# Layer 1's experts in a four-layer transformer kernel: four of eight chunks routed in 23 blocks instead of dense

## The reference, cut to what matters

```python
def _moe(x, gW, gb, W1, b1, W2, b2):
    xf = x.reshape(-1, d)
    gates = jax.nn.softmax(xf @ gW + gb, axis=-1)
    top2_scores, top2_idx = jax.lax.top_k(gates, 2)
    w = (jax.nn.one_hot(top2_idx, NUM_EXPERTS, dtype=xf.dtype) * top2_scores[..., None]).sum(1)
    h = jax.nn.relu(jnp.einsum('nd,edf->enf', xf, W1) + b1[:, None, :])
    y = jnp.einsum('enf,efd->end', h, W2) + b2[:, None, :]
    out = jnp.einsum('ne,end->nd', w, y)
```

## Time and profile before

| | us |
|---|---|
| timed runs, median (lowest to highest of 3) | 2776.42 (2775.82 to 2781.66) |
| profiled execution, its own time | 2793.7 |
| its span, first to last instruction | 2791.9 |
| TensorE busy | 2617.3 |
| VectorE busy | 2019.3 |
| ScalarE busy | 1664.1 |
| GpSimd busy | 1181.0 |

### The profile page before, as it was taken

The page is one execution under the profiler, slowest core; times in us unless marked ns, Lnnn a source line. Parts: engine busy times, 40 slices in busy tenths (PEclk is TensorE's granted clock), DMA queues, the critical chain, the costliest instruction groups (busy, mean ns, idle before and its releaser), DMA issues.

```text
span 2791.9 us, 67999 instructions
## 1 busy us (share of the span) xinstructions
PE 2617.3 (94%) x24870; PEld 1792.3 (64%) x24870; DVE 2019.3 (72%) x5620; ACT 1664.1 (60%) x4107; POOL 1181.0 (42%) x1620
## 2 busy tenths in 40 slices
PE   5999999998889999999997999999989988999898
PEld 2666666666577666676665555677767765666676
DVE  6988888876544666666666998556678876887675
ACT  3888888884234767777765777543335544334665
POOL 6888888853601566211113454122333321014441
PEclk9999999999999999999999999999999999999999
DMA  3012222112275122111113544000054432435650
GB/s 113 17 54 76 76 75 67 54 37 85 89 219 158 30 45 45 32 39 30 26 32 105 185 136 134 1 1 16 15 160 147 129 92 63 92 78 158 201 165 28
DMA packets 218857, 230.81 MB, mean 83 GB/s; under 512 B 18608, under 2 KB 188272, under 8 KB 216480
## 3 DMA queue, kind: packets, MB, share of 16 engines
q1 hardware_dynamic: 212000, 207.58, 26.9%
q10 hardware_dynamic: 3456, 12.58, 1.4%
q0 software_dynamic: 3072, 6.30, 0.7%
HBM read 165.87 MB, written 75.60 MB: 86 GB/s over the span
## 4 chain that ended last, share of the span: by engine, by line
PE 72%; DVE 12%; ACT 7%; issue 4%; POOL 2%; DMA 2%; SPq 1%; ACTq 0%; another core or an unknown queue 0%; DVEq 0%; POOLq 0%
PE pb L163 64%; ACT big L967 4%; PE pb L663 3%; ACT big L160 2%; DVE big L3015 2%; DVE big L837 2%; PE pb L596 2%; DVE big L236 1%; PE pb L2986 1%; DVE big L3520 1%; PE pb L249 1%; DVE big L820 1%; DVE big L747 1%; POOL hs L1854 1%; DVE big L179 0%
## 5 line engine op out<-in xcount | busy, mean ns | idle before, releaser
L163 PE MATMUL pb<-big 128*128 128x128 f32 (+12 forms) x19624 | 2352.2, 327 | 102.3 <-DVE big L3015 34.5
L163 PEld LDWEIGHTS pb<-big 64*128 64x128 bf16 (+4 forms) x19624 | 1481.4, 144 | 760.4 <-issue 430.8
L160 ACT ACTIVATE big<-pb 128x512 f32<-128x512 f32 (+7 forms) x1481 | 846.4, 620 | 555.1 <-PE pb L163 295.9
L160 ACT ACTIVATE big<-pb,big 128x512 f32<-128x512 f32 (+2 forms) x502 | 276.1, 585 | 426.9 <-PE pb L163 353.7
L3015 DVE TENSOR_REDUCE big<-pb 128x4 f32<-128x1024 f32 (+1 forms) x256 | 277.6, 1087 | 71.4 <-PE pb L163 66.8
L967 ACT ACTIVATE big<-big 128x256 f32<-128x256 f32 x512 | 253.8, 499 | 67.7 <-DVE big L842 66.7
L967 ACT ACTIVATE big<-pb,big 128x128 f32<-128x128 f32 (+1 forms) x512 | 256.8, 527 | 60.1 <-DVE big L822 59.8
L837 DVE CUSTOM_DVE_ANT_0 big<-pb,big 128x256 f32<-128x256 f32 x512 | 186.7, 422 | 96.9 <-PE pb L163 93.6
L187 POOL TENSOR_SCALAR big<-big 128x4 f32<-128x4 f32 (+2 forms) x102 | 26.7, 262 | 542.2 <-DVE big L182 542.1
L174 POOL TENSOR_TENSOR big<-big 128x128 f32<-128x128 f32 x168 | 74.5, 457 | 346.6 <-DVE big L171 346.5
L1046 POOL TENSOR_TENSOR big<-big 128x512 f32<-128x512 f32 x128 | 159.7, 1275 | 139.8 <-DMA big<-recip 139.8
(11 more groups left out here) (211 smaller groups left out, 2452.9 us busy)
## 6 DMA issues: line engine op xcount, KB each, us to landing
parts<-big SPq DMA_DIRECT2D x384, 96.0 KB, 2.5
big<-parts SPq DMA_DIRECT2D x72, 512.0 KB, 4.1
big<-recip SPq DMA_DIRECT2D x128, 256.0 KB, 5.3
big<-comb SPq DMA_DIRECT2D x32, 512.0 KB, 8.0
hs<-in_zero SPq DMA_DIRECT2D x10, 1472.0 KB, 9.1
big<-in_wx SPq DMA_DIRECT2D x31, 450.0 KB, 4.3
parts<-big SPq DMA_DIRECT2D x192, 64.0 KB, 2.1
big<-parts ACTq DMA_DIRECT2D x24, 512.0 KB, 4.6
```

The source lines that it names most:

```text
L160: return e.activation(o, i, f, bias=bias, scale=scale)
L163: return e.matmul(o, l, r_, start=start, stop=stop, skip_group_check=True)
```

## The change

Layer 1's experts become a stage of their own, `routed_ffn`: chunks 0 and 1 dense (units 0 to 15), chunks 2 to 5 routed as 23 blocks of 256 rows (steps 16 to 38), chunks 6 and 7 dense (steps 39 to 54). The routed rows come straight from X1. Ranking and table run beside the first pair, 32 scatters in steps 2 to 13. The table of experts sets which weights a block fetches from a new input `wx1` (642 columns, laid out by expert on the host). Two rows per routed token are gathered from `ys` by `late_ffn_fetch`, 28 of 32 gathers beside the last pair and four in layer 2's attention; `late_ffn_vector`, `late_ffn_scalar` and `late_ffn_gpsimd` combine, normalize and add them four tiles at a time, in steps 45/46 and 49/50 and in steps 2/3 and 12/13 of layer 2's attention. Layer 2's first steps are hosted from step 48 of 55 instead of 55 of 64.

```diff
+        def late_ffn_fetch(e, g):
+            m, k, i = g // 4, g % 4 // 2, g % 2
...
+            if g % 4 == 0 and m >= 3:
+                e.wait_ge(ffn_added, m - 2)
+            t = 2 * m + i
+            at = HOME1[t // 8][:, 8 * k + t % 8:8 * k + t % 8 + 1]
+            e.indirect_dma_start(out=CHOSEN1[m % 3][:, k, i, :], out_offset=None, in_=dr["ys"],
+                                 in_offset=bass.IndirectOffsetOnAxis(ap=at, axis=0)).then_inc(chosen_in[m % 3], 16)
+        def late_ffn_vector(e, c):
...
+            for i, a in enumerate(rows):
+                n = 4 * c + i
+                x = e.scalar_tensor_tensor(out=a[:, 0, :], in0=a[:, 0, :], scalar=SHARE1[:, 0, n:n + 1], in1=X1[:, 8 + n, :],
+                                           op0=ALU.mult, op1=ALU.add)
...
+        def late_ffn_scalar(e, c):
+            e.wait_ge(ffn_rstd, c + 1)
+            for i in range(4):
+                a = CHOSEN1[(2 * c + i // 2) % 3][:, 0, i % 2, :]
+                x = act(e, a, a, ACT.Identity, LNMR[:, i:i + 1], LRS[:, i:i + 1])
+            x.then_inc(ffn_normed, 1)
+        def late_ffn_gpsimd(e, c):
+            e.wait_ge(ffn_mean, c + 1)
...
+            e.tensor_tensor(LRS, LRS, EPS[:, 0:4], ALU.pow).then_inc(own.sem, own.up())
...
+            e.wait_ge(ffn_normed, c + 1)
+            two = lambda a: a.unsqueeze(1).to_broadcast([128, 2, 128])
+            for m in (2 * c, 2 * c + 1):
+                a, b = CHOSEN1[m % 3][:, 0], 4 + m
+                for w, op in ((two(LNW[:, 256:384]), ALU.mult), (two(LNW[:, 384:512]), ALU.add), (two(GA[:, b, 128:256]), ALU.mult)):
+                    e.tensor_tensor(a, a, w, op).then_inc(own.sem, own.up())
+                    e.wait_ge(own.sem, own.n)
+                e.tensor_tensor(X[:, 2 * b:2 * b + 2, :], X[:, 2 * b:2 * b + 2, :], a, ALU.add).then_inc(ffn_added, 1)
+        def routed_ffn():
+            k, E = 1, 8
+            DENSE, ROUTED = (0, 1, 6, 7), (2, 3, 4, 5)
+            NB1 = 23
+            T0, T1 = 16, 16 + NB1
+            T = T1 + 16
...
+            modulated_at, guests_at = T0 + 12, T - 7
...
+            scatters = {t: [(m, three[m % 3]) for m in range(3 * (t - first), min(3 * (t - first) + 3, 16))]
+                        for first in (2, 8) for t in range(first, first + 6)}
+            gathers = {T1 + 1 + 2 * m + i: range(4 * m + 2 * i, 4 * m + 2 * i + 2) for m in range(7) for i in range(2)}
+            combined_at = {T1 + 6: 0, T1 + 10: 1}
...
+            def tensor_block_up(e, j):
...
+                for f in range(2):
+                    t = mm(e, bk[:, 256 * f:256 * f + 256], WB[J % 4][:, 128 * f:128 * f + 128], HTB[J % 3], True, True)
...
+            def vector_block_down(e, j):
+                y, J = slots["y", T0 + j], NBLK + j
+                bk = empty(e, y)
+                e.wait_ge(y_stored[J % 2], 16 * (J // 2))
+                e.tensor_tensor(YB[J % 2], bk[:, 0:256].rearrange("p (k c) -> p k c", k=2),
+                                WB[J % 4][:, 514:642].unsqueeze(1).to_broadcast([128, 2, 128]), ALU.add).then_inc(y.free, 1)
...
+                e.wait_ge(table_made, 2)
+                for j in range(4):
+                    sync_weights(e, j)
+                e.wait_ge(scattered, 16 * (48 + 32))
+                for j in range(4):
+                    sync_rows(e, j)
+                for j in range(NB1 + 1):
+                    if 1 <= j and j + 3 < NB1:
+                        sync_rows(e, j + 3)
+                    if 1 <= j and j + 3 < NB1:
+                        sync_weights(e, j + 3)
+                    if j >= 1:
+                        sync_store(e, j - 1)
...
         in narrow_attention, k == 2:
-                    found += [(c, piece) for at, piece in (((2, "normed0"), (4, "normed1"), (7, "turn")) if b % 2 else
-                                                           ((2, "stats0"), (4, "stats1"))) if at == i]
+                                                           (((5, "stats0"), (6, "stats1")) if causal else ((2, "stats0"), (4, "stats1")))) if at == i]
+                return [(c, p) for c, first in ((2, 2), (3, 12)) for p, at in (("sum", 0), ("norm", 1)) if causal and first + at == t]
+                    if causal and t in (5, 6):
+                        for g in range(18 + 2 * t, 20 + 2 * t):
+                            late_ffn_fetch(e, g)
-                    if k == 2 and b == 5:
-                        e.wait_ge(gated, 8 + 32 * (k - 1))
+                    if k == 2 and b == 11:
+                        e.wait_ge(ffn_added, 8)
+                        e.wait_ge(gated, 24)
                         second_gates(e, k)
-                 moe(1, 8, X1A.rearrange("p (t c) -> p t c", c=128)), narrow_attention(2), ...
+                 routed_ffn(), narrow_attention(2), ...
```

680 lines of the change are left out of this document (658 added, 22 removed).

## The result

The changed kernel took 2790.61 us in the median of seven runs (2785.56 to 2798.59), the kernel before 2777.87 us beside it (2772.55 to 2781.66). The ratio is 1.0049, 95% interval 1.0035 to 1.0063: 13 us slower, clearly told from no change. Measured again later beside other runs of before it was 1.0062 (1.0046 to 1.0079). The forecast was 2769 us, 7 us less than before; the sign was wrong, the time lies inside the range. Its chances were 0.49 for faster and 0.31 for slower.

What follows compares the result with a forecast made beforehand. TensorE alone was taken to set the pace. Terms: -124.3 + 57.5 + 8 + 5 - 6 + 7 + 24 + 21.5 = -7.3 us, from the median 2776.42 to 2769 us; 8-in-10 range 2740 to 2796.

Steps and rivals of the forecast that it cites:

- At nothing: List of edits put at no cost: shared own-semaphores, moved statistics, later load of the second gates, host's table of weights.
- The blocks: Layer 1's 23 routed blocks: 2.5 us each, 57.5 us, plus 5 for gates of chunks 6 and 7 holding VectorE.
- the pieces: Transposes and gate logits of chunks 6 and 7, 6 us, said to fit into TensorE's spare time beside the blocks: -6.
- the store loop of 2.5 us: Layer 1's blocks: with two buffers YB, eviction waits for the store of two blocks earlier, setting 2.5 us a block.
- Rival 2: Blocks at layer 0's pace, store landing at 4.3 us or more, 2.8 to 3.1 us a block; chance 0.28.
- Rival 3: Stores land near 1.8 us, blocks run at TensorE's 2.0 us, 11.5 us less, 2757 us; chance 0.07.
- The first block: Hand-over to the routed blocks: last scatter 5 us too late, 2 more at low clock, +7 us; ends 0 and 11.
- The join: Last dense pair to layer 2's first score: TensorE stands 24 us behind GpSimd's 45 us of work; ends 14 and 30.
- Rival 1: GpSimd's queue is hidden: the 24 us and half of layer 2's loss don't appear, 2735 or 2741 us; chance 0.20.
- Layer 2's early steps: Layer 2's attention: late normalizations, sums and gathers delay negated maxima, splits and exponentials, +21.5 us; ends 10 and 30.
- the blocks' 71 us: Upper end for layer 1's 23 blocks, at 3.08 us each, layer 0's own pace after its first wait.
- GpSimd's 30: Upper end of TensorE's wait for GpSimd's work beside the last dense pair, forecast at 24 us.

Runs made afterwards that it cites:

- gates_load_late: Changed kernel with the load of the next layer's gates issued after the last block's store; ratio 1.0038 to the kernel before.
- three_buffers: Changed kernel with three result buffers YB instead of two in layer 1's blocks; ratio 1.0067 to the kernel before.
- one_multiply: Changed kernel without the product with ln2's weight and the sum with its bias in each late normalization; ratio 1.0020 to the kernel before.
- late_spread: Changed kernel, statistics back in steps 2 and 4, layer 2's two late combinations in steps 22 to 28 and 38 to 44, last gathers in 32, 33; ratio 1.0030 to before.
- after_again: The changed kernel unaltered, measured once more as a control; ratio 1.0062 to the kernel before.
- undone_and_moved: Changed kernel, statistics back in steps 2 and 4, chunk 0's finish behind the last scatter, gates' load behind the last block; ratio 0.9973 to the kernel before.

## Why the prediction was wrong

**The step that failed** stands under "At nothing": "the statistics moved from steps 2 and 4 to 5 and 6 (read only in the next group of eight)". I asked who reads the moved result and found nobody in haste. I did not ask what the moved instructions stand ahead of. They lengthen TensorE's wait for a row maximum by 0.66 us in every second group (1.20 instead of 0.54); and the root that follows them waits on GpSimd, ahead of a split on whose way the next batch's parts are. The cost was 9 us in the changed kernel's steady part (175.5 against 166.4; undoing it gave 8.9 back), 6 to 10 in time, and 17 in the kernel before.

**A load that I didn't count.** The gates' load of 1 MB stands on SyncE's queue in the middle of the blocks. It was in the program before, beside dense units, and cost nothing that the trace shows. Among blocks it made TensorE wait for rows: 5 to 8 us (gates_load_late). The prediction named no such term.

**The blocks.** 57.5 + 5 us were forecast for 23 blocks and the gates' work on VectorE. Measured are 70.0 us for 22 intervals, 64.7 without the gates' load, with the pieces in it that I thought hidden. So the size was nearly right for a wrong reason: the store loop of 2.5 us does not bind (three_buffers), TensorE alone needs 2.34, and small waits for rows of 0.2 to 1 us and the pieces fill the rest. Rival 2, the store's landing at its 4.3 us as the pace, falls. Rival 3 was right that TensorE and not the store paces the blocks, but not at 2.0 us and not because stores land quickly. By the rule that I had cited (the Trainium skill, "DMA: Bandwidth & Descriptors", section "Anatomy of one DMA") a store lands in 2.3 us, an estimate: the page gives its figures for a DMA issued from GpSimd, and these stores are SyncE's. The list of DMA issues of the changed kernel has a median of 3.8 for ys over both layers, so the row stays above the rule, and neither sets the pace.

**The first block.** Forecast 7 us (5 and 2 of clock), ends 0 and 11; a wait of 9.89 us, with the clock at 0.61 in the 4 us behind it. With that the term was too small by some 4 us. Moving the finish gained 4. The mechanism was right: GpSimd's scatters and chunk 0's finish fill it up to 1834.6, and the first rows come behind them. The first dense unit starts 1.9 us later after layer 1's attention than before (12.55 against 10.63 us behind its last transposes), with transposes and gate logits of a later chunk now ahead of it.

**The join.** Forecast 24 us of waits, measured 9.55 + 3.04 + 2.21 + 8.45 = 23.25. one_multiply shows that GpSimd's queue sets its end. Rival 1, the hidden queue, falls.

**Layer 2's early steps.** Forecast 21.5, measured 61.6 - 40.0 = 21.6; late_spread shows by taking the work away that it was all of it. That the number fits so closely is in part luck: the terms were waits alone, and of the 21.6 us 16 are waits and 5 TensorE's longer busy time at the lower granted clock, which no term had.

So of the forecast's -7.3 us, layer 1's experts gained 21 us up to the first score in the profiled execution (248.3 against 269.7) and 15 in after_again (254.5) instead of 29 (with chunk 0's finish and the gates' load moved, in undone_and_moved, it is 30: 240.1), the early steps lost 22 and 20, and the statistics took 9 more behind them. That makes the kernel 9 and 14 us slower up to the 24th transposes, where 13 and 17 were timed over the whole kernel; the rest is within what two executions differ. Both large terms that I had worked out at length were right within 1 us. What decided the sign were an edit that I had passed over in a sentence and a transfer that I had not named at all.

**The range.** The measured time lies inside it only by its wide upper end. 2796 us is not where the two ends meet that the prediction names: the blocks' 71 us and GpSimd's 30 give 2769 + 13.5 + 6 = 2788.5, below the measured 2790.61. Only with the end of 30 for layer 2's attention as well is it 2797.

**Left open:** why the moved statistics cost 17 us in the kernel before but 6 to 10 in the changed one; and whether the queue or the DMA engines hold the row load behind the megabyte.

## What to carry to other kernels

An instruction that moves costs by what stands behind it in its engine's queue, not only by who reads its result: for each moved one look at the next instruction on that engine, and on every engine that must answer it in between (here a root on GpSimd ahead of a split). When a stage changes from computing on data that is there to streaming it, look again at every transfer that its queue already carried. And work that is due much later than it is made should stand away from the filling of the next pipeline, with each engine's share placed by itself and a waiting one never ahead of the stage's own rhythm: the same two combinations cost 22 us in steps 2 to 13 and 8 us where they stood last.
